# Two stage boundaries of a graph and mixture-of-experts kernel: scatters moved behind a boundary, blocks released by an earlier count, work re-ordered at both

## What is computed

```python
x = x + _L0_gnn_ref(_layernorm(x), adj, ...)   # adj @ (x @ weight) + bias
x = x + _L0_ffn_ref(_layernorm(x), ...)        # attention, then top-2 of 8 experts
x = x + _L1_gnn_ref(_layernorm(x), adj, ...)   # the same with degrees normalised
x = x + _L1_ffn_ref(_layernorm(x), ...)        # top-2 of 6 experts
# the experts of _L0_ffn_ref
probs = jax.nn.softmax(flat @ router_w.T, axis=-1)
tp, ti = jax.lax.top_k(probs, TOPK)
for e in range(NE):
    hh = jax.nn.silu(flat @ w1[e].T) * (flat @ w3[e].T)
    out = out + weights[:, e:e + 1] * (hh @ w2[e].T)
```

## Time and profile before

| | |
|---|---|
| median of 3 runs | 906.34 us (905.11 to 907.66) |
| the profiled execution | 905.17 us, its span 903.3 us |
| TensorE | 846.2 us busy, 94%, mean granted clock 0.983 |
| VectorE | 725.7 us, 80% |
| ScalarE | 552.2 us, 61% |
| GpSimd | 433.1 us, 48% |
| transfers | 105.90 MB, mean 117 GB/s |

### The profile page before, as it was taken

The page is one execution under the profiler, slowest core; times in us unless marked ns, Lnnn a source line. Parts: engine busy times, 40 slices in busy tenths (PEclk is TensorE's granted clock), DMA queues, the critical chain, the costliest instruction groups (busy, mean ns, idle before and its releaser), DMA issues.

```text
span 903.3 us, 23489 instructions
## 1 busy us (share of the span) xinstructions
PE 846.2 (94%) x6650; PEld 678.3 (75%) x6651; DVE 725.7 (80%) x2848; ACT 552.2 (61%) x1167; POOL 433.1 (48%) x425
## 2 busy tenths in 40 slices
PE   4799999999964999999999999899999999999998
PEld 4688888988753999999999998555655555555563
DVE  4489999999864798777777788788888888888863
ACT  2488998998852556566665653455555555555554
POOL 3127888888777910230020020766655566656300
PEclk9899999999996999999999999999999999999999
DMA  5402222123113766666666661333333344343322
GB/s 166 116 21 66 62 65 73 52 70 108 42 43 106 222 165 166 170 186 168 172 175 167 176 162 45 117 112 115 116 117 111 112 132 137 141 125 118 100 82 93
DMA packets 102317, 105.90 MB, mean 117 GB/s; under 512 B 27022, under 2 KB 86304, under 8 KB 100080
## 3 DMA queue, kind: packets, MB, share of 16 engines
q1 hardware_dynamic: 91808, 86.36, 32.8%
q0 software_dynamic: 8784, 18.16, 6.5%
q10 hardware_dynamic: 1664, 0.66, 0.3%
HBM read 79.90 MB, written 25.23 MB: 116 GB/s over the span
## 4 chain that ended last, share of the span: by engine, by line
PE 58%; DVE 3%; issue 3%; DMA 2%; ACT 1%; POOL 1%; DVEq 0%; SPq 0%; ACTq 0%; POOLq 0%
PE banks L2193 16%; PE banks L2230 10%; PE banks L2353 8%; PE banks L2345 8%; PE banks L2321 6%; PE banks L2205 2%; PE banks L2262 2%; PE banks L2288 2%; PE banks L2251 1%; PE banks L2279 1%; DMA slots_out<-ys 1%; PE banks L2367 1%; PE banks L2297 1%; PE banks L2241 1%; PE banks L2271 1%
## 5 line engine op out<-in xcount | busy, mean ns | idle before, releaser
L1517 POOL DMA_INDIRECT expert_rows<-slots_out,slot_c x128 | 146.7, 1146 | 88.7 <-DVE ys L1752 55.0
L368 POOL DMA_INDIRECT slots_in<-flat,slot_now x120 | 121.0, 1009 | 34.5 <-issue 34.2
L2193 PE MATMUL banks<-xT_hi,w_hi 128*128 128x256 f32 (+1 forms) x426 | 126.3, 297 | 0.4 <-DVE w_lo L1769 0.4
L2193 PE MATMUL banks<-xT_hi,w_lo 128*128 128x256 f32 (+1 forms) x426 | 120.4, 283 | 0.0
L2193 PE MATMUL banks<-xT_lo,w_hi 128*128 128x256 f32 (+1 forms) x426 | 120.0, 282 | 0.0
L2230 PE MATMUL banks<-w_sb,prod 128*128 (+1 forms) x852 | 107.9, 276 | 3.8 <-DVE ys L1752 3.8
L2230 PEld LDWEIGHTS banks<-w_sb,prod 128*128 128x128 f32 (+1 forms) x852 | 102.0, 192 | 4.5 <-issue 4.4
L2193 PEld LDWEIGHTS banks<-xT_hi,w_hi 128*128 128x128 f32 (+1 forms) x426 | 75.6, 178 | 0.6 <-issue 0.6
L2193 PEld LDWEIGHTS banks<-xT_lo,w_hi 128*128 128x128 f32 (+1 forms) x426 | 76.1, 179 | 0.0
L2193 PEld LDWEIGHTS banks<-xT_hi,w_lo 128*128 128x128 f32 (+1 forms) x426 | 75.8, 178 | 0.0
L1575 ACT ACTIVATE w_hi<-w_raw 128x684 fp32r<-128x684 f32 x71 | 54.9, 773 | 30.1 <-PE banks L2193 26.3
(11 more groups left out here) (310 smaller groups left out, 2393.5 us busy)
## 6 DMA issues: line engine op xcount, KB each, us to landing
gate_bc<-gates_dram SPq DMA_DIRECT2D x16, 1536.0 KB
w_raw<-in_w SPq DMA_DIRECT2D x71, 342.0 KB, 3.3
xs<-slots_in SPq DMA_DIRECT2D x71, 128.0 KB, 2.7
slots_out<-ys SPq DMA_DIRECT2D x71, 128.0 KB, 3.2
base_all<-in_x SPq DMA_DIRECT2D x16, 256.0 KB, 3.1
out<-ob SPq DMA_DIRECT2D x16, 256.0 KB, 2.7
slots_in<-zrow SPq DMA_DIRECT2D x20, 128.0 KB, 3.3
adjt<-in_adj_t SPq DMA_DIRECT2D x32, 64.0 KB
```

Of the source, the lines that this page charges most:

```text
L368: G.indirect_dma_start(out=slots_in, out_offset=bass.IndirectOffsetOnAxis(ap=slot_now0[p][:, n:n + 1], axis=0), in_=flat[p][:, n // 2, :], ...
L1517: G.indirect_dma_start(out=rows[p][:, n, :], out_offset=None, in_=slots_out[0:filled(g) * R, :], in_offset=bass.IndirectOffsetOnAxis(ap=sl ...
L2193: last = T.matmul(banks[bank][0:m, half * R:(half + 1) * R], ww[:, par, n * HIDP + c * P:n * HIDP + c * P + m], xx[:, par, :], start=q == ...
```

## The change

Group 14's scatters are moved behind the boundary beside those of group 15. `full` and `due` are made at group 13 (`EARLY`) from the counts through group 12, for both semaphores, and SP reads them into registers ahead of the boundary. The weights of block 0 are split in the last steps of stage 1. SP writes all eight zero fills, ScalarE none. The store of block 1 is put ahead of block 8's waits. TensorE has three filling matmuls instead of eight at the first boundary and none at the second. At the second boundary the order of `f3T(0)`, `lo(0)`, `add1(1)`, `f3_(1)` and `xb_(1)` is changed.

```diff
+            EARLY = NG - 3
+            due_groups = ((EARLY + 1) // 2, EARLY // 2)
...
             def but_last(g):
-                return None if isinstance(g, int) and g == NG - 1 else g
+                return None if isinstance(g, int) and g >= NG - 2 else g
...
+                    sp.wait_ge(early_due, 3)
+                    for p, groups in enumerate(due_groups):
+                        for k in range(NE0):
+                            due_at[p].append(sp.value_load(due[0:1, p, k:k + 1], min_val=16 * 2 * TG * groups, max_val=16 * TG * NG))
...
                         f_(g[3])
+                        if isinstance(g[5], int) and g[5] == NG - 1:
+                            act.wait_ge(ld_wr[0], 16)
+                            S.activation(w_hi[:, 0, :], w_raw[:, 0, :], ACT.Copy).then_inc(w_hi_done, 1)
                         ssq(g[5])
...
+                            if isinstance(g, int) and g == EARLY:
+                                V.tensor_scalar(full[:, :], banks[B_RANK][0:1, 64:72], float(R), -1.0, ALU.is_ge, ALU.mult).then_inc(early_due, 1)
+                                dve.wait_ge(early_due, 1)
+                                for p, groups in enumerate(due_groups):
+                                    V.tensor_scalar(due[:, p, :], full[:, :], 16.0 * 2 * TG * (NG // 2 - groups), 16.0 * TG * NG,
+                                                    ALU.mult, ALU.add).then_inc(early_due, 1)
...
                         st1(g[1])
+                        if isinstance(g[4], int) and g[4] == NG - 1:
+                            dve.wait_ge(w_hi_done, 1)
+                            V.tensor_tensor(w_lo[:, 0, :], w_raw[:, 0, :], w_hi[:, 0, :].bitcast(f32), ALU.subtract).then_inc(w_lo_done, 1)
                         ssv_(g[4])
...
-                    link(V.tensor_scalar(full[:, :], banks[0][0:1, 8:16], float(R), -16.0 * 2 * TG, ALU.is_ge, ALU.mult))
-                    link(V.tensor_scalar(due[:, :], full[:, :], 16.0 * TG * NG, None, ALU.add))
...
                     def block_of(k, u):
+                        if isinstance(k, int) and k == NE0:
+                            result_of(k - 7, u - 7)
                         if live(k, 0):
-                            if isinstance(k, int) and k == 0:
-                                sp.wait_ge(scattered[0], 16 * TG * NG)
                             if isinstance(k, int) and k < NE0:
-                                value = sp.value_load(due[0:1, k:k + 1], min_val=16 * 2 * TG * (NG // 2 - 1), max_val=16 * TG * NG)
                                 row = k * REG * R
                             else:
                                 if isinstance(k, int) and k == NE0:
                                     sp.wait_ge(tabled, TABLE + 2)
-                                    sp.wait_ge(zero_fill, 16 * (NDUM + NE0 + NE0 // 2))
-                                    sp.wait_ge(zero_fill2, 16 * (NE0 // 2))
-                                    sp.wait_ge(scattered[1], 16 * TG * NG)
+                                    sp.wait_ge(zero_fill, 16 * (NDUM + NE0 + NE0))
+                                    for p in range(2):
+                                        sp.wait_ge(scattered[p], 16 * TG * NG)
                                 row = row_of(k)
...
-                                sp.wait_ge(scattered[1], value)
+                                for p in range(2):
+                                    sp.wait_ge(scattered[p], due_at[p][k])
...
-                        if isinstance(k, int) and k in (3, 5):
-                            zero_rows(k - 3)
-                            zero_rows(k - 2)
+                        if isinstance(k, int) and 3 <= k < 6:
+                            for e in ((0, 1, 2, 3), (4, 5), (6, 7))[k - 3]:
+                                zero_rows(e)
...
-                        for n in range(2 * TG):
+                        for m in range(4 * TG):
+                            p, n = m // (2 * TG), m % (2 * TG)
                             G.indirect_dma_start(
...
                         if isinstance(g[1], int) and g[1] == 1:
                             rstd0(1)
+                            xb_(1)
...
                         var1(later(g[2], 1))
+                        if isinstance(g[2], int) and g[2] == 1:
+                            f3_(1)
                         add0(later(g[1], 2), p[1])
-                        f3_(later(g[2], 1))
+                        f3_(later(g[2], 2))
                         add1(later(g[1], 2), p[1])
                         ob_(g[4])
-                        lo(g[2], p[2])
+                        lo(later(g[2], 1), p[2])
...
                             f3_(0)
+                        elif k == LOOPED + 12:
+                            lo(0, 0)
                             add1(1, 1)
-                        elif k == LOOPED + 12:
+                        elif k == LOOPED + 13:
                             st0(1)
...
+                            if isinstance(g, int) and g == 0:
+                                pe.wait_ge(y_copied, NBLK)
...
                     def block_and_first(k, u):
-                        block_of(k, u)
                         if isinstance(k, int) and k == NBLK + 1:
                             f3T(0)
-                    fill_up(8)
+                        block_of(k, u)
+                    fill_up(3)
                     blocks(pe, block_and_first, 2)
-                    fill_up(2)
                     sweep(pe, body)
```

More of the change, by code:

```diff
@@ L1554, in body @@
                         gt(4, g[0], p[0])
-                        xb_(g[1])
+                        xb_(None if isinstance(g[1], int) and g[1] == 1 else g[1])
                         gt(5, g[0], p[0])
@@ L1564, in _ @@
                     S.preload_act_table(ACT.Silu)
-                    for e in range(NE0 // 2, NE0):
-                        row = act.value_load(fill[0:1, e:e + 1], min_val=0, max_val=ROWS - R)
-                        act.dma_start(two_tiles(row), zrow[:, :].unsqueeze(1).broadcast_to([P, 2, C])).then_inc(zero_fill2, 16)
                     def weight_hi(k, u):
@@ L1577, in block_of @@
                     def block_of(k, u):
-                        if isinstance(k, int) and k == 0:
-                            weight_hi(0, 0)
                         if live(k, 0):
```

34 lines of the change are left out of this document (21 added, 13 removed).

## The result

The changed kernel takes 912.83 us in the median of five runs (910.92 to 920.42) against 906.17 (905.11 to 907.66) for the kernel before beside it: ratio 1.0093, 95% interval 1.0066 to 1.0121; the two medians by themselves lie 0.7% apart. It is slower, and outside the range I gave. The ratios, with their intervals, need not be the quotients of the medians beside them.

The account below looks back on a forecast made before the run. TensorE, busy 94% of the span, was taken as the bound, leaving only the two stage boundaries: 1.3 + 0.2 = 1.5 us off 905.17 gives 903.7, or 904.8 as median; range 899.8 to 907.8.

Parts of the forecast that it names:

- The drain: End of the first stage: earlier power, logits read and counts open the next stage at 280.4, 2.77 us earlier.
- The first block: Behind the first boundary: 6 filling passes instead of 16, first expert product at 285.0, 7.15 us earlier.
- What gives way: First boundary: sixteen scatters delay block 8's load, block 2's store and block 5's product; 1.3 of 7.15 us stay gained.
- the landing: Block 2's store, issued at 309.1, was taken to land after 6.5 us, at 315.6.
- My bounds: Landing times of such a store: 3.4 us outside a stretch of large weight loads, 7.65 us within one.
- My estimate from it: If SP's queue gets half of the transfer engines, block 2's store lands in about 4 us; first boundary gains 3.8.
- The second boundary: Reordering starts the router product some 4 us earlier, but GpSimd's gathers set the next meeting point; net 0.2 us gained.
- The wait of 3.6 us: Second boundary: the 4 us saved in front become a wait ahead of group 1's transposes.
- D: Rival: sixteen scatters in a row drag, the last landing 7 us later; 911.8 us; chance 0.08.
- E: Rival: first boundary opens no earlier, held by SP's register loads or the last chain; 907.6 us; chance 0.08.
- B: Rival: block 2's store lands in 3.4 to 4 us, first boundary gains 3.8 to 4.4; 902.0 us; chance 0.26.
- C: Rival: group 2's gathers begin before 565.5, so the second boundary keeps 3.3 us; 901.7 or 899 us; chance 0.10.

Follow-up runs that it names:

- g1: Kernel before with only the change's new order at the second boundary, timed again; 906.41 us, ratio 1.0015 to the kernel before.
- f3: Changed kernel with the old second-boundary order and group 14's eight scatters back in the first stage; 901.07 us, ratio 0.9921 to the kernel before.
- g4: Changed kernel with group 14's scatters back in the first stage and the gates broadcast held behind group 2's gathers; 902.06 us, ratio 0.9961 to the kernel before.
- g5: Changed kernel with group 14's eight scatters back in the first stage, new second-boundary order kept; 903.43 us, ratio 0.9973 to the kernel before.
- e1: Kernel before with only the change's new order at the second boundary, first timing; 911.87 us, ratio 1.0054 to the kernel before.
- g2: Kernel before with the new second-boundary order and the gates broadcast held behind group 2's gathers; 907.42 us, ratio 1.0009 to the kernel before.
- f1: The changed kernel timed a third time, unaltered; 915.93 us, ratio 1.0091 to the kernel before.
- e2: Changed kernel with the old order at the second boundary; 911.16 us, ratio 1.0042 to the kernel before.
- e0: The changed kernel timed once more, unaltered; 915.95 us, ratio 1.0097 to the kernel before.
- f2: Changed kernel with unused filler matmuls in TensorE's waits in the last two steps of the first stage; 916.77 us, ratio 1.0113 to the kernel before.
- h1: Repeat of f3 on a slower chip; 952.48 us, ratio 0.9966 to the kernel before.
- e7: Kernel before with the new second-boundary order and the gates broadcast held behind group 2's gathers, slower chip; 953.87 us, ratio 1.0012 to the kernel before.
- e3: Changed kernel with the old second-boundary order and GpSimd's weight loads held until 12 results are copied; 904.62 us, ratio 0.9969 to the kernel before.
- h2: h1 with GpSimd's weight loads held behind the copy of block 11, slower chip; 948.95 us, ratio 0.9959 to the kernel before.
- f4: Changed kernel with late GpSimd weight loads, held gates broadcast and filler matmuls; 907.39 us, ratio 1.0008 to the kernel before.
- e6: Kernel before with only GpSimd's weight loads held behind the copy of block 11, slower chip; 950.02 us, ratio 0.9981 to the kernel before.

## Why the prediction was wrong, point by point

**The drain: wrong.** I had the boundary open 2.77 us earlier. The step that failed is "the logits end at 272.6, so VectorE reads them at 272.7 instead of 274.9: 2.2 us earlier". It took the logits' 1.23 us from the earlier trace rows, an execution in which the clock fell only during them. In every other profile of either first stage, but for the two with fillers, they ran at half clock, 1.94 us, and TensorE's part then ends with GpSimd's: in g1, which has the first stage of before, GpSimd's scatters stand ahead of the power just the same (it ends at 278.29) and cost 0.1 us, since the logits end at 278.17. From the start of the last logits to the opening g1 takes 10.47 us (276.23 to 286.70), the changed kernel 10.16. The change buys 0.2 to 0.3 us there, not 2.77. In the earlier trace rows the same distance is 11.85. The early `full` and `due` did shorten VectorE's own chain from the logits on (6.3 to 5.7 us), but the opening does not follow: with group 14's scatters back in place (f3, g4, g5) the distance is 10.38 to 10.39, the same as with the old counts (e1, g2).

The rest is how long the step before it takes, and when the clock falls in it. The opening is 3.0 us late: group 14's logits start 1.1 later than in the profile of before, the step from them to group 15's takes 3.7 more, and 1.7 come back behind. TensorE in the kernel before, for group 14, then in g1 and in f1 (L1171 and L1190 are the logits of groups 14 and 15):

```profile
260.32 1.08 PE L1171 MATMUL banks<-rws,f2T 128*128 128x64 f32 x8 [1.16 <-ACT f2T L497]
```

```profile
261.46 1.73 PE L1171 MATMUL banks<-rws,f2T 128*128 128x64 f32 x8 [1.17 <-ACT f2T L497]
276.23 1.94 PE L1171 MATMUL banks<-rws,f2T 128*128 128x64 f32 x8 [0.78 <-ACT f2T L497]
```

```profile
260.73 1.07 PE L1190 MATMUL banks<-rws,f2T 128*128 128x64 f32 x8 [1.16 <-ACT f2T L506]
273.20 1.94 PE L1190 MATMUL banks<-rws,f2T 128*128 128x64 f32 x8 [0.78 <-ACT f2T L506]
```

Where it falls by 263, the step takes 14.6 to 14.9 us, where it falls near 266, 12.5, and in the profile of before, where it fell near 272, 11.0. On the faster chips an early fall stands in two of the four profiles with the old first stage (g1, g2) and in six of the eight with the new one and no fillers. So it comes without the change; whether the change makes it more frequent, by the early counts that stand some 6 us ahead of it (255.46 in the changed kernel), so few profiles do not settle.

**The first block: right.** From the opening to the first product I had 4.6 us; it takes 4.91 (before 8.95, and 7.37 in e1, whose filling ran partly at full clock). This is what f3 keeps.

**What gives way: right in mechanism, mis-sized.** Sixteen scatters at 0.97 us each, block 8's load, the store of block 2 behind it, the copy of VectorE, the wait of TensorE, the fallen clock behind it: all there. At block 5's product the miss is 7.3 us (316.35 forecast, 323.63 measured): 4.0 stand ahead of the store's issue, 3.3 in its landing. The term that failed is the landing, 6.5 us forecast, 9.76, 9.94 and 9.60 measured (changed kernel, e2, f1; 9.72 and 9.31 in e0 and f2). My bounds were 3.4 and 7.65. I had the store 2.6 us behind the first of the large weight loads (384 KB; six small ones go ahead of it), as good as the 3.1 of before; it is issued 0.76 to 0.78 us behind it in all five. The missing 1.8 us are two small terms: I counted the last scatter's 2.3 us from its end and not from its start, and gave SP 4.6 us from there to the store where it takes 3.8. By and large the landing follows that distance in all profiles that have such a store in their chain: 0.06 us ahead 6.92 (g5), 0.11 behind 9.55 (h1), 0.76 to 1.19 behind 9.3 to 9.9, 1.81 behind 8.15 (g4), 2.31 behind 8.34 (e7), 2.80 behind 7.92 (g2), 3.14 behind 7.65. No run moved the distance by itself, but g1, with the old first boundary, has the long landing too, 1.14 us behind:

```profile
304.49 9.93 DMA slots_out<-ys
```

The Trainium skill's "DMA: Bandwidth & Descriptors", section "Queues, rings and completion order", has the queues sharing the engines packet by packet. My estimate from it was 4 us. The trace disagrees with that estimate by more than twice; with the loads gone it is 3.83 (e3). And the landing is not the whole loss: e3 takes 6.5 us away and block 5 still waits 4.69, f3 takes 7 to 10, since the load of block 8 and the store behind it then come early.

**The second boundary: a step was missing.** I shifted the gathers by 0.9 us and stopped there. What I did not ask is which transfer they then meet. In the kernel before the broadcast came 2.9 us behind the last gather (576.72 to 579.58); with the new order it comes 0.03 to 1.65 us behind. The wait of 3.6 us that I named ahead of the transposes of group 1 is there with 2.02, for the reason given. "The low part then follows both adds and ends as late as before" failed: the adds wait for the gathers, and the low part with them.

**The rivals.** D (scatters drag) did not happen: sixteen take 0.97 to 1.05 each, 21.1 us in all. The warning of the Trainium skill's "SBUF — State Buffer", section "SBUF: two separate sides", stands all the same, and my reading that scatters beside the split of weights are not lengthened came from where they happened to start. Nine other profiles (f1, e1, e3, f3, g1, g4, g5, h1, h2) have scatters that start 0.11 to 0.66 us behind the start of the split; all of them are lengthened, to 1.04 to 1.60 us, and end some 0.85 us behind the split's end. VectorE's and GpSimd's timelines in f1:

```profile
292.88 0.86 DVE L1792 TENSOR_TENSOR w_lo<-w_raw,w_hi 128x684 fp32r<-128x684 f32 x1
```

```profile
293.09 1.50 POOL L1495 DMA_INDIRECT slots_in<-flat,slot_now  x1 [0.30 <-issue]
```

In f1 this makes the sixteen 0.9 us longer, 22.0, far from the 4.2 that D needed. E's outcome, a boundary that does not open earlier, is what happened, by the step's length and the logits at half clock; SP's register loads are not shown to have a part in it. B and C did not happen.

## What to carry to other kernels

A step that is moved takes its DMAs past other queues: list for each of them what it will stand beside, and how far apart the two were before. A distance of 3 us between two transfers can be what keeps them apart. And a wait that one profile shows between two chains that end close together is not a gain: ask what the other chain takes at the other clock. The best kernel here keeps the other pieces of the first boundary, among them shorter filling and the earlier split of the first weights, and leaves the scatters where they were (0.992 on one chip, 0.997 with an interval up to 1.0002 on another).

## What the runs showed of the hardware

- A 128 KB store issued by SP lands in 3.8 to 3.9 us with GpSimd's weight loads out of the way (e3, f4), in 7.65 us issued 3.1 us behind the first 384 KB load, in 6.92 issued beside it (g5), and in 9.3 to 9.9 us issued 0.76 to 1.19 behind it (seven profiles).
- A 1.5 MB broadcast issued within 0.33 us behind the last of eight indirect gathers brings that gather's landing from 2.5 to 2.6 us to 6.5 to 7.4.
- A scatter of GpSimd that starts 0.11 to 0.66 us into VectorE's split of the weights takes 1.04 to 1.60 us in place of 0.97.
- The same kernel took 953 us on two chips and 906 to 907 on the others. In the slower ones TensorE is busy for 88 of 100 us in the first stage where it was for 99.8, VectorE's longest waits there again having no releaser on the core (in e6). The two rows are e6's waits of VectorE from 100 to 200 and its window:

```profile
DVE rden L687 <- remote: 12.7, 6, 3.8
```

```profile
100.00:200.00 100.00, 88.48 (x1088) 77.00 (x1088) 83.79 (x403) 75.63 (x205) 68.22 (x70) 0.95 0.18 53
```

The cause was not tried.
